# Layers 0 and 1: query and key score stacks kept in rows of 512 bytes, the keys stored three times in DRAM and loaded in one transfer

## The reference, cut to what matters

```python
x = x + tanh(g_xattn[l]) * attention(layernorm(x), ctx)

def attention(query, ctx):            # layers 0 and 1
    q = heads(query @ Wq.T + bq)      # 16 heads of 8
    k = heads(ctx @ Wk.T + bk)
    v = heads(ctx @ Wv.T + bv)
    # layer 0 only: q, k = rope(q), rope(k)
    scores = einsum('bhsd,bhtd->bhst', q, k) / sqrt(8)
    attn = softmax(scores, axis=-1)
    out = einsum('bhst,bhtd->bhsd', attn, v)
    return merge(out) @ Wo.T + bo
```

## Time and profile before

| | us |
|---|---|
| median of 3 runs (1620.72 to 1637.18) | 1624.66 |
| the profiled execution's own time | 1634.38 |
| its span, first to last instruction | 1632.6 |
| PE busy | 1399.9 (86%) |
| DVE busy | 869.3 (53%) |
| ACT busy | 551.7 (34%) |
| POOL busy | 396.9 (24%) |

### The profile page before, as it was taken

The page is one execution under the profiler, slowest core; times in us unless marked ns, Lnnn a source line. Parts: engine busy times, 40 slices in busy tenths (PEclk is TensorE's granted clock), DMA queues, the critical chain, the costliest instruction groups (busy, mean ns, idle before and its releaser), DMA issues. The chain is left out here.

```text
span 1632.6 us, 26439 instructions
## 1 busy us (share of the span) xinstructions
PE 1399.9 (86%) x8933; PEld 868.7 (53%) x8933; DVE 869.3 (53%) x2519; ACT 551.7 (34%) x1291; POOL 396.9 (24%) x713
## 2 busy tenths in 40 slices
PE   5899987985799968996994995665999999999998
PEld 2577663543577745564884674442444344444443
DVE  5667646875476533332664343764446546446435
ACT  2366656642577542223552231440101011001001
POOL 3677411104566200001355122611000000000000
PEclk9799998995699788996776898886999999999999
DMA  6675730005667439100001111232202303302200
GB/s 188 164 161 135 161 81 1 0 1 121 127 164 168 108 122 418 54 0 24 22 29 32 49 55 46 62 125 104 104 27 84 111 1 110 110 2 110 104 7 13
DMA packets 74722, 143.03 MB, mean 88 GB/s; under 512 B 13431, under 2 KB 53879, under 8 KB 64743
## 3 DMA queue, kind: packets, MB, share of 16 engines
q1 hardware_dynamic: 68038, 133.89, 28.0%
q0 software_dynamic: 3296, 6.76, 1.4%
q10 hardware_dynamic: 3264, 0.79, 0.3%
HBM read 99.33 MB, written 41.09 MB: 86 GB/s over the span
## 5 line engine op out<-in xcount | busy, mean ns | idle before, releaser
L2704 DVE TENSOR_TENSOR l3f_weighted_T<-l3f_w_e,l3f_xnT 128x512 f32<-128x512 f32 x128 | 88.3, 691 | 129.4 <-PE psum L2455 115.3
L2455 PE MATMUL psum<-l3f_weighted_T,w_l3f_q 128*128 128x512 f32 x256 | 133.7, 604 | 15.9 <-DVE l3f_weighted_T L2704 14.1
L2455 PE MATMUL psum<-l3f_weighted_T,w_l3f_k 128*128 128x512 f32 x256 | 131.6, 596 | 0.0
L2455 PE MATMUL psum<-l3f_weighted_T,w_l3f_v 128*128 128x512 f32 x256 | 131.4, 595 | 0.0
L2464 PE MATMUL psum<-l3f_weighted_T,w_l3f_o 128*128 128x512 f32 x256 | 124.3, 625 | 1.7 <-DVE l3f_weighted_T L2704 1.7
L702 DVE TENSOR_REDUCE l1x_minus_max<-psum 128x4 f32<-128x512 f32 x128 | 85.0, 687 | 72.5 <-PE psum L362 70.2
L2704 DVE TENSOR_TENSOR l3f_weighted_T<-l3f_w_e,l3f_oT 128x512 f32<-128x512 f32 x128 | 88.4, 692 | 57.2 <-PE psum L2464 30.0
L702 DVE TENSOR_REDUCE l0x_minus_max<-psum 128x4 f32<-128x512 f32 x128 | 84.1, 686 | 35.4 <-PE psum L362 33.8
L111 POOL TENSOR_TENSOR l3f_ln_rstd<-l3f_ln_mean_var,eps 128x4 f32<-128x4 f32 x8 | 2.0, 244 | 355.4 <-DVE l3f_ln_mean_var L104 355.4
L2464 PEld LDWEIGHTS psum<-l3f_weighted_T,w_l3f_o 128*128 128x128 f32 x256 | 39.3, 188 | 82.8 <-DVE l3f_weighted_T L2704 78.1
L524 ACT ACTIVATE l0x_probsT<-psum 128x512 f32<-128x512 f32 x128 | 73.0, 597 | 27.3 <-PE psum L375 26.1
(11 more groups left out here) (500 smaller groups left out, 2973.7 us busy)
## 6 DMA issues: line engine op xcount, KB each, us to landing
l3f_w_e<-l3f_weights_scratch SPq DMA_DIRECT2D x32, 1024.0 KB, 4.7
sorted_x<-zeros SPq DMA_DIRECT2D x1, 16896.0 KB, 59.3
l0x_k_stack<-l0x_k_scratch SPq DMA_DIRECT2D x48, 192.0 KB
l0x_q_stack<-l0x_q_scratch SPq DMA_DIRECT2D x48, 192.0 KB
l1x_k_stack<-l1x_k_scratch SPq DMA_DIRECT2D x48, 192.0 KB
l1x_q_stack<-l1x_q_scratch SPq DMA_DIRECT2D x48, 192.0 KB
w_l2f_w<-in_l2f_w SPq DMA_DIRECT2D x2, 2048.0 KB, 13.5
l0x_k_scratch<-l0x_k_parts SPq DMA_DIRECT2D x16, 192.0 KB, 6.0
```

What stands on the lines that cost most here:

```text
L2455: ins = pe.matmul(bank[:, :], w[name][:, e, :], xe[:, e % 2, :], start=(e == 0), stop=(e == NE3 - 1))
L2704: dve.tensor_tensor(xe[:, e % 2, :], wE[:, g % 2, e, :], src, ALU.mult).then_inc(s_xe, 1)
```

## The change

The three DRAM copies and the layout change; the engines' arithmetic, the number of matmuls and LEAD stay. The scratch tensors hold whole rows of 512 tokens; the key parts are stored three times over (`b` in 0..2), so that one DMA of 72 rows loads a half of the key stack; the query parts are stored once, and the same 24 rows are loaded three times. A half is now 256 of 512 tokens in each (row, head), so every piece of a load is 512 bytes long. One semaphore instead of two counts what is stored, so a half's load waits for the whole store.

```diff
-        blocks = {"k": NPART, "q": 2 * NPART - 1}
-        scratch = {n: nc.dram_tensor(f"{name}_{n}_scratch", (2, 2, blocks[n], P, HALF), BF16).ap() for n in "kq"}
-        stack = {n: sb(f"{n}_stack", [TROWS, 2, 2, HEADS, HALF], BF16) for n in "kq"}
+        scratch = {"k": nc.dram_tensor(f"{name}_k_scratch", (2, NPART, NPART, P, T), BF16).ap(),
+                   "q": nc.dram_tensor(f"{name}_q_scratch", (2, NPART, P, T), BF16).ap()}
+        stack = {n: sb(f"{n}_stack", [TROWS, 2, HEADS, T], BF16) for n in "kq"}
...
-        loads = {"k": NPART, "q": NPART}
-        stores = {"k": 1, "q": 2}
+        loads = {"k": 1, "q": NPART}
+        stores = {"k": NPART, "q": 1}
...
             def store(n, g):
 
                 sp.wait_ge(s_parts[n], g + 1)
-                for hf in range(2):
-                    to = scratch[n][g % 2, hf].rearrange("a p t -> p a t")
-                    sp.dma_start(to[:, 0:NPART, :], parts[n][:, :, half(hf)]).then_inc(s_stored[n][hf], 16)
-                    if n == "q":
-                        sp.dma_start(to[:, NPART:2 * NPART - 1, :], parts["q"][:, 0:NPART - 1, half(hf)])\
-                          .then_inc(s_stored["q"][hf], 16)
+                if n == "k":
+                    for b in range(NPART):
+                        sp.dma_start(scratch["k"][g % 2, :, b].rearrange("a p t -> p a t"), parts["k"][:, :, :])\
+                          .then_inc(s_stored["k"], 16)
+                else:
+                    sp.dma_start(scratch["q"][g % 2].rearrange("b p t -> p b t"), parts["q"][:, :, :])\
+                      .then_inc(s_stored["q"], 16)
 
             def load(n, g, hf):
 
-                parts_stored(sp, n, g, hf)
+                parts_stored(sp, n, g)
                 if g >= 2:
                     sp.wait_ge(s_T, 4 * (GS * (g - 2) + 2 * hf + 2))
-                rows_of = lambda ap: ap.rearrange("a (d h) t -> (a d) (h t)", h=HEADS)
-                block_rows = NPART * HD
-                for s in range(NPART):
-                    first = s if n == "q" else 0
-                    sp.dma_start(stack[n][s * block_rows:(s + 1) * block_rows, g % 2, hf, :, :]
-                                 .rearrange("r h t -> r (h t)"), rows_of(scratch[n][g % 2, hf, first:first + NPART]))                      .then_inc(s_stack[n][g % 2][hf], 16)
+                if n == "k":
+                    sp.dma_start(stack["k"][0:SROWS, g % 2, :, half(hf)],
+                                 scratch["k"][g % 2].rearrange("a b (d h) t -> (a b d) h t", h=HEADS)[:, :, half(hf)])\
+                      .then_inc(s_stack["k"][g % 2][hf], 16)
+                else:
+                    rows_of_a = NPART * HD
+                    for a in range(NPART):
+                        sp.dma_start(stack["q"][a * rows_of_a:(a + 1) * rows_of_a, g % 2, :, half(hf)],
+                                     scratch["q"][g % 2].rearrange("b (d h) t -> (b d) h t", h=HEADS)[:, :, half(hf)])\
+                          .then_inc(s_stack["q"][g % 2][hf], 16)
...
-                act.dma_start(stack["q"][SROWS:TROWS, g % 2, c // 2, :, of_seq(c)], mT[:, seq(c)]).then_inc(s_mrow[c], 16)
+                act.dma_start(stack["q"][SROWS:TROWS, g % 2, :, seq(c)], mT[:, seq(c)]).then_inc(s_mrow[c], 16)
```

More of the change, by code:

```diff
@@ L232, in heads_attention @@
         s_split = sem("split_step")
-        s_stored = {n: [sem(f"{n}_parts_in_dram_{hf}") for hf in range(2)] for n in "kq"}
+        s_stored = {n: sem(f"{n}_parts_in_dram") for n in "kq"}
         s_stack = {n: [[sem(f"{n}_stack_in_{p}_{hf}") for hf in range(2)] for p in range(2)] for n in "kq"}
@@ L255, in heads_attention, with parts_stored @@
         half = lambda hf: slice(hf * HALF, (hf + 1) * HALF)
-        of_seq = lambda c: slice((c % 2) * P, (c % 2 + 1) * P)
-        loads = {"k": NPART, "q": NPART}
-        stores = {"k": 1, "q": 2}
+        loads = {"k": 1, "q": NPART}
+        stores = {"k": NPART, "q": 1}
         def stack_landed(eng, n, g, hf):
             eng.wait_ge(s_stack[n][g % 2][hf], 16 * loads[n] * (g // 2 + 1))
-        def parts_stored(eng, n, g, hf):
-            eng.wait_ge(s_stored[n][hf], 16 * stores[n] * (g + 1))
+        def parts_stored(eng, n, g):
+            eng.wait_ge(s_stored[n], 16 * stores[n] * (g + 1))
         block = ctx.enter_context(nc.Block())
@@ L272, in _ @@
             sp.wait_ge(s_fill, 4)
-            sp.dma_start(stack["k"][SROWS:TROWS, :, :, :, :].rearrange("a p f h t -> a (p f h) t"),
-                         bcast(ones_row[:, 0:HALF].unsqueeze(1), [NPART, 4 * HEADS, HALF])).then_inc(s_ones, 16)
+            sp.dma_start(stack["k"][SROWS:TROWS, :, :, :].rearrange("a p h t -> a (p h) t"),
+                         bcast(ones_row[:, :].unsqueeze(1), [NPART, 2 * HEADS, T])).then_inc(s_ones, 16)
             def store(n, g):
                 sp.wait_ge(s_parts[n], g + 1)
-                for hf in range(2):
-                    to = scratch[n][g % 2, hf].rearrange("a p t -> p a t")
-                    sp.dma_start(to[:, 0:NPART, :], parts[n][:, :, half(hf)]).then_inc(s_stored[n][hf], 16)
-                    if n == "q":
-                        sp.dma_start(to[:, NPART:2 * NPART - 1, :], parts["q"][:, 0:NPART - 1, half(hf)])\
-                          .then_inc(s_stored["q"][hf], 16)
+                if n == "k":
[5 more added lines that the diff above has]
+                      .then_inc(s_stored["q"], 16)
@@ L361, in scores @@
                     h = 4 * u + i
-                    ins = pe.matmul(bankS[u % 2][:, seq(i)], stack["q"][0:SROWS, g % 2, c // 2, h, of_seq(c)],
-                                    stack["k"][0:SROWS, g % 2, c // 2, h, of_seq(c)], start=True, stop=True)
+                    ins = pe.matmul(bankS[u % 2][:, seq(i)], stack["q"][0:SROWS, g % 2, h, seq(c)],
+                                    stack["k"][0:SROWS, g % 2, h, seq(c)], start=True, stop=True)
                 ins.then_inc(s_S, 1)
@@ L374, in scoresT @@
                     h = 4 * u + i
-                    ins = pe.matmul(bankT[u % 2][:, seq(i)], stack["k"][:, g % 2, c // 2, h, of_seq(c)],
-                                    stack["q"][:, g % 2, c // 2, h, of_seq(c)], start=True, stop=True)
+                    ins = pe.matmul(bankT[u % 2][:, seq(i)], stack["k"][:, g % 2, h, seq(c)],
+                                    stack["q"][:, g % 2, h, seq(c)], start=True, stop=True)
                 ins.then_inc(s_T, 1)
@@ L609, in split @@
                     step(pool.tensor_tensor(full[n][:, :], turned[n][0][:, :], turned[n][1][:, :], ALU.add))
-                for hf in range(2):
-                    parts_stored(pool, n, g - 1, hf)
+                parts_stored(pool, n, g - 1)
                 p = [parts[n][:, a, :] for a in range(NPART)]
```

## The result

The changed kernel is slower. In the first comparison it took 1637.46 us (median of 9 runs, 1631.86 to 1646.06) against 1626.15 us (median of 9, 1614.71 to 1637.18): a ratio of 1.0078 with a 95% interval of 1.0049 to 1.0107. A second comparison gave 1.0106 (1.0069 to 1.0144). I had forecast 1613 us and a range of 1602 to 1638; the loss of some 13 to 17 us has the other sign than the forecast's gain of 12. The first median, 1637.46, lies at the very edge of the range and the second, 1645.06, outside it.

A forecast was written before the change was run, and what follows sets the result against it. PE was taken to set the pace, with the DMA loads near a tie. Maxima -6.2, clock -3 and group 1 -3 sum to -12.2 us, so 1624.7 - 12 = 1613 us; range 1602 to 1638.

The forecast's parts named there:

- Maxima behind small pieces: PE's waits for the maxima's DMA, 4.60 and 1.58 us, vanish once load pieces are 512 bytes: -6.2 us.
- rival 1: Maxima's DMA stays as late as now because a queue keeps its turn for several pieces: about 1623 us, chance 0.22.
- Stores: A group's stores grow to 1573 kB, 4.5 us at 350 GB/s against 3.6, all beside PE work in steady state.
- Loads: A group's 2359 kB of stack loads run at 150 GB/s in 512-byte pieces; nothing counted for the 72-row transfer.
- Does it stay hidden?: Steady groups: loads and stores fit 21.9 us in layer 1 if loads reach 144 GB/s; 0.7 us spare at 150, cost 0.
- Group 1 of layer 1: The wait of group 1's first scores for its stack shrinks, -3.8 to -1.0; taken as -3 us.
- Clock: Layer 1's main-loop entry: without the two waits the granted clock rises after 5 us of unbroken work, -3 us (0 to -5).
- Rival 3: Loads get faster, 170 GB/s or more, by the 72-row transfer; group 1's and group 7's waits go: 1604 us, chance 0.16.
- Group 7: Waits before the last group's first scores, 3.13 and 1.69 us, stay: 0, with ends -4.8 and +4.
- Start of each layer: First scores slip up to 3 us behind longer key stores, hidden by POOL's chain: 0, at worst +2.
- Rival 2: 512-byte loads are slower and DMA becomes the bound at first scores of groups 2 to 7: 1630 to 1660 us, chance 0.20.

The follow-up runs named there:

- e1: The kernel before with only the stacks' rows cut to 512 bytes, stores by halves and three key transfers kept: 1.0023 of the kernel before.
- e10: The kernel before with keys and queries both stored three times, each stack loaded in one 72-row transfer, 8 KB rows, halves apart: 0.9976 of the kernel before.
- e9: The kernel before with each stack loaded from single copies by one 72-row transfer, outermost count 24, 8 KB rows: 0.9883 of the kernel before.
- e16: The same kernel as e9, run again in another set: 0.9904 of the kernel before.
- e2: The kernel before with keys stored three times by halves and loaded in one transfer, queries stored in three blocks, 8 KB rows: 0.9937 of the kernel before.
- e6: e2 with its one key load split into three transfers of 24 rows, each from its own copy: 1.0023 of the kernel before.
- e12: e2 with 512-byte rows in the keys' stack only, the queries' rows staying 8 KB: 0.9990 of the kernel before.

## Why the prediction was wrong, point by point

- **Maxima behind small pieces (-6.2): right in size, doubtful in mechanism.** The waits are 0 in the changed kernel and in e1. PE reads sequence 1's maxima 12.3 us after their issue in layer 1 (422.42 to 434.76), without a wait, against 19.6 before. That excludes rival 1 there, but shows at most 12.3 us and not the "under 1 us". In layer 0 it reads them 17.2 us after issue (53.40 to 70.60) against 13.0 before, so there the missing wait alone shows nothing; in e1 it is 11.3 us without a wait. And 8 KB pieces need not be slow: e10 has no such wait, e9 none in layer 1 (read 10.9 us after issue), e16, the same kernel, 1.2 us there. A turn of one 8 KB piece for each 256-byte piece can't be the whole story.
- **Stores (350 GB/s, hidden): the rate was fair, the cover not.** The stretch below holds only key stores and runs at 345 GB/s. What I missed is where they stand: between the second half's loads and the next group's, so that a late group's key load follows its key store by 9.7 to 11.4 us (groups 3 to 7 of layer 1) where it was 7.8 to 8.6.

```profile
391.00:393.00 2.00, 1.22 (x3) 0.50 1.03 345
```

- **Loads (R = 150): the number was right, and it was the wrong comparison.** Alone they run at 142 to 147 GB/s, a group's in 16.0 to 16.6 us, where the cover left 16.4. "The small pieces alone need not slow them" was wrong: it took the 28 ns of a stored piece for a loaded one. With one transfer and 8 KB rows the loads do 195 to 200, so the short rows cost a quarter of that rate. And "I count nothing" for the 72-row transfer threw away a gain of 10 us that keys x3 has by itself (e2, e6). The Trainium skill's swizzle rule that I had set beside it ("SBUF — State Buffer", Door 1: The DMA port swizzle) would have made key loads up to 1.6 times faster; the trace shows 195 to 200 against 158, 1.25 times, at an unchanged share, so it had the direction for the keys. No run shows its ports to be the reason, and the queries' 188 and 194 by 24-row transfers don't fit it as I had worked it out.
- **"Does it stay hidden?": this is the step that failed.** It asked for 144 GB/s and found 0.7 us of room at 150. The short rows' 142 to 147 GB/s already use up that room; behind them stands the term for the whole store, put at 1 us a group (0 to 2) and with cost 0. The engines stand nearly still for 3 us after the two late stores shown, and the runs price the wait, behind the tripled store, at 10 to 11 us over both layers (0.0060, 0.0065, each plus or minus 0.0045 to 0.005), and the short rows at 13. The sum had 0 for both. Periods went from 20.8 to 21.5, 22.0 and 25.8 us, PE's own waits counted in. The sum treated the store's 4.5 us, the landing and the loads as work that could be laid end to end without gaps; each gap between them is time in which the engines idle and the loads wait.
- **Group 1 of layer 1 (-3): right**, 0.23 us are left. **Clock (-3): partly.** It is back at 1.00 from 437 us, 2.6 us after what my 425 becomes with layer 1's later start (+9.4). But after three of the six stalls of 2 to 6.5 us shown above it fell anew: those of 5.49, 3.31 and 6.52 us (half speed from about 201.5 to 218.5, 519 to 522 and 563.5 to 570). The sum had no such term. It let the clock rise after 5 us of unbroken work, but from 206 to 218 us PE is busy all 12 us and the clock stays at half. Rival 3 put about 1.5 us of lost clock behind each of group 7's waits, where the stretches before show half speed for some 3 and 20 us of busy PE.
- **Group 7 (0, -4.8 to +4): outside its end.** 5.49 and 6.52 us against 3.13 and 1.69: +7.2.
- **Start of each layer (0, at worst +2): wrong.** First scores came 2.6 us later in layer 0 and 3.6 in layer 1 (beyond its later start), and group 1 of layer 0 waits 4.53 us, which I had not priced. That is near the +3 a layer given for the case without cover. POOL's chain hid some: the wait at the first turned maxima fell from 3.52 to 1.00 us. SP, which I had put at 0, is part of it. Group 0's six query loads, 2.37 us to issue before, now block SP for 4.78 us, and one transfer of group 1 for 5.43 us:

```profile
32.69 4.78 SPq L298 DMA_DIRECT2D l0x_q_stack<-l0x_q_scratch  x6
38.57 2.14 SPq L280 DMA_DIRECT2D l0x_k_scratch<-l0x_k_parts  x3
53.01 0.79 SPq L292 DMA_DIRECT2D l0x_k_stack<-l0x_k_scratch  x1
58.27 5.43 SPq L298 DMA_DIRECT2D l0x_q_stack<-l0x_q_scratch  x1
```

- **The rivals.** Rival 2 had the right sign and half of the place: of the 26.6 us of stack waits 16.1 stand at groups 2 to 7 and 10.5 at groups 0 and 1. It hung them on a rate below 144 GB/s, which is only just met; its 1630 to 1646 hold both medians, and they are why the range reached 1638, so that the first median fell inside is no merit of the sum. Rival 3's one transfer of 72 rows did gain in e2, and the rest of the change covered it.

With the runs' terms in place of mine: -10 for keys x3, +13 for the short rows (the maxima's gain already within), +11 for the wait for the whole, +14 in all; measured were +12.7 and +17 (0.0078 and 0.0106 of 1626). They were measured on kernels between the two and contain the clock's share, which no run sets apart.

## What to carry to other kernels

When the DMA engines and PE are near a tie, price a change of transfers by three things apart: how fast a transfer of this shape runs alone, what has to land before it may start, and what stands between them in the issuing queue. A dependency on a longer store costs its gap as well as its bytes. Two changes that are cheap alone (a longer store; a wait for all of it) can be dear together, so build them together before adding their prices. Where pieces are long already, ask for one transfer instead of three, with an outermost count that still splits over many engines; that was worth about 17 us here without moving one byte more.

## What the runs showed of the hardware

- A transfer whose source has an outermost count of 3 showed a share of 0.20 (75 GB/s), about three of 16 engines; 8 KB rows with an outermost count of 24 or 72 showed 0.72 to 0.79, about twelve.
- Pieces of 512 bytes load into SBUF at 142 to 147 GB/s with the engines at a share of 0.91 to 0.92, where 8 KB pieces do 158 to 200 at 0.72 to 0.79. Stores of 512-byte pieces run at 288.
- With 8 KB rows one transfer of 72 rows moved 195 to 200 GB/s. Three of 24 from one copy moved 158 for the keys before and 194 for the queries in e2, at the same share. Why is open.
- After a wait of PE of 1.7 to 6.5 us the granted clock fell to half, during the wait or right behind it, in five places of the two profiles (3.13 and 1.69 us before; 5.49, 3.31 and 6.52 changed) and stayed there for some 3 to 20 us of busy PE; the spell after the shortest wait, 1.69 us, was the longest.
- Stall for stall, 1 us of a late stack cost less than 1 us of the program in some kernels (e12: 20.6 us of waits, 0.9990; e1: 17.8 us, 1.0023): the waits rank the kernels only roughly.
